# Another order for the last chunks of a layer stack, and another way through the "weighted values" stage, in a seven-part transformer kernel

## The reference

```python
x = x + attn_a(ln(x))        # softmax(x x^T) x over 2048 tokens
x = x + ffn(ln(x))           # 2 layers: local attention + gated feed-forward
x = x + attn_b(ln(x))        # "weighted values"
x = x + ffn(ln(x))           # the same 2 layers, the same weights

def attn_b(x):
    q, k, v = split(x @ qkv_w)                       # 128 columns each
    mq, mk  = mean(q), mean(k)                       # per token
    s_qk, s_q2, s_k2 = sums of products of (q-mq), (k-mk) / 127
    A = (((2*mq*mk+c1)*(2*s_qk+c2)) / ((mq**2+mk**2+c1)*(s_q2+s_k2+c2)+1e-7))**2
    h = relu(groupnorm(conv3(A), 2 groups of 2 channels) * gn_g + gn_b)
    A = A + conv3(h) + conv2_b
    weights = softmax(sigmoid(A), over tokens)
    ch_w = sigmoid(relu(mean_tokens(x) @ ch_w1 + ch_b1) @ ch_w2 + ch_b2)
    return (weights[..., None] * v * ch_w) @ proj_w + proj_b
```

## Time and profile before

| what | us |
|---|---|
| median of 3 runs (range) | 1821.97 (1821.23 to 1822.14) |
| the profiled execution, its own time | 1820.76 |
| its span, first to last instruction | 1819.0 |
| TensorE, VectorE, ScalarE, GpSimd busy in the span | 1613.2, 1284.9, 1202.6, 1175.3 |
| mean granted TensorE clock, as a share of 2.4 GHz | 0.945 |

### The profile page before, as it was taken

How to read it: one execution, slowest core, us unless ns; L and a number is a source line. 1 busy time by engine, 2 the same in 40 slices (tenths; PEclk the granted TensorE clock), 3 DMA queues, 4 the chain that set the end, 5 groups by cost and what they waited for, 6 DMA issues and landing times.

```text
span 1819.0 us, 47842 instructions
## 1 busy us (share of the span) xinstructions
PE 1613.2 (89%) x20074; PEld 1259.1 (69%) x20074; DVE 1284.9 (71%) x1689; ACT 1202.6 (66%) x1870; POOL 1175.3 (65%) x772
## 2 busy tenths in 40 slices
PE   4999978999999999999866666999999999999974
PEld 2777847877777777777644544877777777777763
DVE  4776658888787878788724455988787877888841
ACT  5876855677677776667655435677767777776753
POOL 3010028988888888888633115988888888888842
PEclk8999988999999999999986577999999999999997
DMA  3100002222222222222100001222222222222111
GB/s 91 41 8 1 1 23 53 65 57 55 51 55 48 58 48 62 49 51 55 31 9 1 0 6 37 68 54 58 49 60 52 55 57 49 57 49 53 42 28 46
DMA packets 66145, 78.87 MB, mean 43 GB/s; under 512 B 14146, under 2 KB 41868, under 8 KB 65932
## 3 DMA queue, kind: packets, MB, share of 16 engines
q1 hardware_dynamic: 65932, 75.82, 17.2%
HBM read 23.10 MB, written 2.10 MB: 14 GB/s over the span
## 4 chain that ended last, share of the span: by engine, by line
PE 61%; ACT 17%; DVE 13%; issue 4%; POOL 3%; DMA 1%; DVEq 0%; POOLq 0%; SPq 0%; ACTq 0%
PE PS L190 9%; PE PS L192 8%; PE PS L191 7%; PE PS L706 7%; PE PS L687 4%; DVE t L976 3%; PE PS L610 3%; PE PS L662 3%; ACT t L900 2%; PE PS L669 2%; ACT L922 2%; ACT L900 2%; DVE t L982 2%; ACT t L846 2%; PE PS L1171 2%
## 5 line engine op out<-in xcount | busy, mean ns | idle before, releaser
L1104 POOL TENSOR_TENSOR t<-t 128x1024 f32<-128x1024 f32 x128 | 427.3, 3339 | 109.9 <-DVE t L982 109.8
L1110 POOL TENSOR_TENSOR t<-t 128x512 f32<-128x512 f32 x256 | 321.6, 1278 | 18.4
L1128 POOL TENSOR_TENSOR HL<-t,HH 114x512 fp32r<-114x512 f32 (+1 forms) x96 | 130.0, 1367 | 141.1 <-ACT HH L906 141.1
L1032 DVE TENSOR_TENSOR yT<-PS,yT 128x128 f32<-128x128 f32 x128 | 37.3, 292 | 234.1 <-PE PS L706 233.8
L190 PE MATMUL PS<-wqh,HH 128*128 128x512 f32 x384 | 175.1, 456 | 30.0 <-DVE t L982 18.2
L846 ACT ACTIVATE t<-PS 128x1024 f32<-128x1024 f32 x128 | 131.3, 1026 | 90.4 <-PE PS L669 90.0
L993 DVE TENSOR_TENSOR t<-t 128x1024 f32<-128x1024 f32 x128 | 183.9, 1437 | 4.5
L814 ACT ACTIVATE t<-PS 128x1024 f32<-128x1024 f32 x128 | 131.2, 1025 | 72.1 <-PE PS L192 72.1
L1003 DVE TENSOR_TENSOR t<-PS,t 128x1024 bf16<-128x1024 f32 x128 | 155.9, 1218 | 19.9 <-ACT t L831 9.1
L976 DVE TENSOR_REDUCE t<-t 128x16 f32<-128x1024 f32 x128 | 154.8, 1210 | 17.1 <-ACT t L814 16.8
L1015 DVE TENSOR_REDUCE t<-PS 128x8 bf16<-128x1024 f32 x128 | 155.6, 1215 | 1.2 <-PE PS L636 1.2
(11 more groups left out here) (219 smaller groups left out, 3872.3 us busy)
## 6 DMA issues: line engine op xcount, KB each, us to landing
t<-t SPq DMA_DIRECT2D x254, 130.0 KB, 2.3
t<-in_c_rope SPq DMA_DIRECT2D x128, 128.0 KB, 2.7
t<-yT SPq DMA_DIRECT2D x112, 128.0 KB, 2.4
t<-in_L_attn_a_x SPq DMA_DIRECT2D x4, 512.0 KB, 6.8
out_x<-t SPq DMA_DIRECT2D x8, 256.0 KB, 2.8
t<-yT SPq DMA_DIRECT2D x16, 127.8 KB, 2.3
t<-in_L_ffn_wqkv SPq DMA_DIRECT2D x2, 768.0 KB, 4.3
t<-in_L_ffn_w SPq DMA_DIRECT2D x2, 341.0 KB, 3.4
```

Of the source, the lines that this page charges most:

```text
L1104: e.e.tensor_tensor(BL.tc.rearrange("p (x h) d -> p x h d", x=2), BL.qn.rearrange("p (x h) d -> p x h d", x=2), sin.to_broadcast([128, 2, ...
L1110: e.e.tensor_tensor(tv[:, :, 32 * s:32 * s + 32], tv[:, :, 32 * s:32 * s + 32], BL.tc[:, :, 32 * (1 - s):32 * (1 - s) + 32], ALU.add).then ...
```

## The change

**Layer stack (both times).** STEPS becomes TS + 4 = 68, and what is left of chunks A, B and Z is written out on each engine in an order of its own, with more banks of PSUM (0 to 7) and with the low halves made by VectorE. The gelu reads the gate from PSUM with its bias, without the copy `gate`. The second matmul waits for each of the three pieces of its operand by itself. The second layer's result is added straight into x1, and the residual add of GpSimd no longer adds that result but yT as it stands after attention; it moves from 17 steps late to 12, and for B and Z behind the loop.

```diff
-        STEPS = 4 * (NC - 1) + 16 + 2
+        STEPS = TS + 4
...
+            def second(C, bank):
-                e.wait_ge(S.ff_lo, 3 * (NC * u + C) + 3)
                 for i in range(3):
+                    e.wait_ge(S.ff_lo, 3 * (NC * u + C) + i + 1)
...
+            second(A, 7)
+            first(B, 2, 1, 6, S.ff_g)
+            first(B, 0, 0, 3, S.ff_l)
+            first(B, 1, 0, 2, S.ff_l)
+            first(B, 2, 0, 0, S.ff_l)
+            centred(Z)
+            second(B, 4)
+            variance(Z, 1)
+            for i, bank in enumerate((3, 2, 0)):
+                first(Z, i, 1, bank, S.ff_g)
+            first(Z, 0, 0, 5, S.ff_l)
+            first(Z, 1, 0, 6, S.ff_l)
+            first(Z, 2, 0, 7, S.ff_l)
+            second(Z, 4)
```

ScalarE's order behind its loop:

```diff
+            gelus(B, range(2))
+            high_for_feed_forward(Z)
+            gelu_there(B, 2, 6)
+            e.e.preload_act_table_set("natural_log_exp_and_others")
+            high_hidden(B, 0)
+            high_hidden(B, 1)
+            square(Z)
+            high_hidden(B, 2)
+            deviation(Z, 1)
+            e.e.preload_act_table_set("gelu_and_others")
+            high_normed(Z)
+            for i, bank in enumerate((3, 2, 0)):
+                gelu_there(Z, i, bank)
+            for i in range(3):
+                high_hidden(Z, i)
```

VectorE's order behind its loop, and GpSimd's residual adds:

```diff
+            add_second(A, 7)
+            e.e.tensor_tensor(fed(HL, Z), BL.ysf, fed(HH, Z).bitcast(F32), ALU.subtract).then_inc(S.sf_lo, 1)
+            gated(B, 0, 3)
+            gated(B, 1, 2)
+            low_hidden(B, 0)
+            gated(B, 2, 0)
+            low_hidden(B, 1)
+            low_hidden(B, 2)
+            scaled(Z)
+            e.e.tensor_tensor(fed(HL, Z), BF.nf, fed(HH, Z).bitcast(F32), ALU.subtract).then_inc(S.nh_lo, 1)
+            add_second(B, 4)
+            gated(Z, 0, 5)
+            gated(Z, 1, 6)
+            low_hidden(Z, 0)
+            gated(Z, 2, 7)
+            low_hidden(Z, 1)
+            low_hidden(Z, 2)
+            add_second(Z, 4)
...
-                if chunk_at(s, 17) is not None and chunk_at(s, 17) >= NCH:
-                    add_residual(chunk_at(s, 17))
+                if chunk_at(s, 12) is not None and chunk_at(s, 12) >= NCH:
+                    add_residual(chunk_at(s, 12))
+            add_residual(NC - 2)
+            add_residual(NC - 1)
```

```diff
-            normed_act(e, 5, 2, 2, x1, False)
+            normed_act(e, 5, 2, 2, x1, 1)
-            normed_dve(e, 5, 2, 2, x1)
+            normed_dve(e, 5, 2, 2, x1, value_weights_dve)
```

```diff
+                    halves(e.e, PS[:, j % 4, 256 * s:256 * s + 256], h, hl, BV.wceh.rearrange("p a b -> p (a b)"),
+                           BV.wcel.rearrange("p a b -> p (a b)"))
+                    mm = halves(e.e, PS[:, 7, 4 * j + 2 * s:4 * j + 2 * s + 2], h, hl, BV.wmh, BV.wml)
...
+            e.wait_ge(S.wv_ch, WVC["relu"])
+            neighbours(BW.h4.rearrange("p a b -> p (a b)"), 4)
+            for c in range(NCH):
+                if c >= 3:
+                    e.wait_ge(S.wv_z, c - 3 + 1)
+                halves(e.e, PS[:, c % 3, :], BW.Mh[c // 4], BW.Ml[c // 4], chunk(HH, c), chunk(HL, c)).then_inc(S.wv_x, 1)
+            e.wait_ge(S.wv_ch, WVC["sums"])
+            e.e.matmul(PS[:, 5, 16:18], avg, sm[:, 22:24], start=True, stop=True, skip_group_check=True).then_inc(S.wv_gm, 1)
+            e.wait_ge(S.wv_ch, WVC["end"])
+            e.wait_ge(S.wv_z, NCH)
+            for c in range(NCH):
+                for j in range(4):
+                    mm = e.e.matmul(PS[:, c, 128 * j:128 * j + 128], BW.w[:, 6, t:t + 1].to_broadcast([128, 128]), ident,
+                                    start=True, stop=True, skip_group_check=True)
```

ScalarE from the first group mean on:

```diff
+            e.e.activation(sm[0:32, 10:12], PS[0:32, 6, 0:2], ACT.Relu, bias=vec[0:32, 8:9], scale=1.0 / N).then_inc(S.wv_sg, 1)
             e.wait_ge(S.wv_cw, 2)
+            e.e.activation(sm[:, 20:22], PS[:, 6, 8:10], ACT.Sigmoid, bias=vec[:, 7:8]).then_inc(S.wv_sg, 1)
             e.e.preload_act_table_set("natural_log_exp_and_others")
+            for b in range(NB):
+                e.e.activation(BW.wpc[b], wp[:, :], ACT.Copy, scale=sm[:, 20 + b:21 + b])
+            e.wait_ge(S.wv_ch, WVC["var"])
+            e.e.activation(sm[:, 24:32], sm[:, 12:20], ACT.Ln, bias=eps_ap, scale=1.0 / 32).then_inc(S.wv_ga, 1)
+            e.e.activation(sm[:, 24:32], sm[:, 24:32], ACT.Exp, scale=-0.5).then_inc(S.wv_ga, 1)
...
+            for c in range(NCH):
+                e.wait_ge(S.wv_x, c + 1)
+                e.wait_ge(S.wv_sum, NCH)
+                e.e.copy(BW.P[c], PS[:, c % 3, :]).then_inc(S.wv_z, 1)
+                if c == 3:
+                    e.wait_ge(S.wv_ch, WVC["ode"])
+                    e.e.activation(w[:, 4, :], w[:, 3, :], ACT.Sigmoid, bias=vec[:, 44:45]).then_inc(S.wv_sg, 1)
+                    e.e.preload_act_table_set("natural_log_exp_and_others")
+                    e.wait_ge(S.wv_sg, 3)
+                    e.e.activation(w[:, 5, :], w[:, 4, :], ACT.Exp).then_inc(S.wv_ex, 1)
```

VectorE's last loop:

```diff
+                    e.wait_ge(S.wv_bs, c + 1)
+                    e.e.tensor_tensor(BW.P[c], PS[:, c, :], BW.P[c], ALU.mult).then_inc(S.wv_pw, 1)
+                if c % 2 == 0 and c:
+                    e.e.tensor_tensor(chunk(x1, c - 1), chunk(x1, c - 1), BW.P[c - 1], ALU.add)
```

More of the change, by code:

```diff
@@ L317, in rest @@
             def rest(c):
-                if twice:
+                if twice is not None:
                     e.wait_ge(S.ln_put, NCH * k + c + 1)
@@ L772, in feed_forward @@
                 if chunk_at(s, 10) is not None:
[L773 removed]
+                    variance(chunk_at(s, 10), 7)
             for s in range(STEPS):
@@ L1161, in weighted_values_pe @@
+        WVC = dict(base=14)
+        WVC["mean0"] = WVC["base"] + 5 + 1
+        WVC["ych"] = WVC["mean0"] + 1
+        WVC["mean1"] = WVC["ych"] + 5
+        WVC["var"] = WVC["mean1"] + 2
+        WVC["relu"] = WVC["var"] + 4
+        WVC["ode"] = WVC["relu"] + 7
+        WVC["sums"] = WVC["ode"] + 1
+        WVC["end"] = WVC["sums"] + 2
+        TT = NB * NT
+        STATS = TT // 2
         def weighted_values_pe(e, stage):
             others_ended(e, stage)
-            TT = NB * NT
-            e.wait_ge(S.wv_w, 3)
@@ L1187, in neighbours @@
                 mm.then_inc(S.wv_nb, 1)
-            sm = BW.sm
+            for j in range(STATS):
+                statistics(j)
+            e.wait_ge(S.wv_dd, STATS)
+            e.e.transpose(PS[:, 0, 0:128], wb[:, 256:384], ident).then_inc(S.wv_v, 1)
             e.wait_ge(S.wv_ch, WVC["base"])
@@ L1272, in build @@
-        WVC["relu"] = WVC["var"] + 4 + 4 + 1
-        WVC["ode"] = WVC["relu"] + 12
-        WVC["chm"] = WVC["ode"] + 2
-        WVC["chr"] = WVC["chm"] + 1
-        WVC["sums"] = WVC["chr"] + 1
-        WVC["end"] = WVC["sums"] + 4
+            for j in range(STATS):
+                dv = BW.dd[j % 3].rearrange("p (a c) b -> p a c b", c=2)
+                e.wait_ge(S.wv_dd, j + 1)
+                e.wait_ge(S.wv_rd, j - 3 + 1)
+                e.e.tensor_tensor(BW.dm[j % 3], dv[:, :, 0, :], dv[:, :, 1, :], ALU.mult).then_inc(S.wv_dm, 1)
@@ new lines, in weighted_values_dve @@
+            follow(v.tensor_tensor(h4, h4, h6, ALU.add))
+            follow(v.tensor_reduce(sm[:, 0:8], cb(h4), AX.X, ALU.add))
+            assert steps[0] == WVC["mean0"]
+            e.wait_ge(S.wv_sum, NCH)
+            follow(v.tensor_reduce(sm[:, 8:10], BW.ysum.rearrange("p (b c) -> p b c", b=NB), AX.X, ALU.add))
+            assert steps[0] == WVC["ych"]
+            e.wait_ge(S.wv_gm, 1)
+            for i in range(2):
+                follow(v.tensor_reduce(four(sm[:, 12:20], i), pair(PS[:, 5, 0:8]), AX.X, ALU.add))
@@ L1352, in weighted_values_dve @@
+            follow(v.scalar_tensor_tensor(cb(h4), eight(sm[:, 12:20]), -1.0 / 32, cb(h4), ALU.mult, ALU.add))
+            follow(v.tensor_tensor(h5, h4, h4, ALU.mult))
+            follow(v.tensor_reduce(sm[:, 0:8], cb(h5), AX.X, ALU.add))
+            assert steps[0] == WVC["mean1"]
+            e.wait_ge(S.wv_gm, 2)
+            for i in range(2):
+                follow(v.tensor_reduce(four(sm[:, 12:20], i), pair(PS[:, 5, 8:16]), AX.X, ALU.add))
             assert steps[0] == WVC["var"]
             e.wait_ge(S.wv_ga, 2)
-            for g in range(2):
-                for b in range(NB):
-                    hv = g5(h4)[:, g, :, b, :]
-                    follow(v.tensor_scalar(hv, hv, sm[:, 12 + 2 * g + b:13 + 2 * g + b], None, ALU.mult))
```

367 lines of the change are left out of this document (182 added, 185 removed).

## The result

The changed kernel takes 1782.0 us (median of 4 runs, 1781.6 to 1782.7), the kernel before 1822.1 us beside it: ratio 0.978 (95% interval 0.9766 to 0.9795), 40.0 us less. The forecast was 1780. The profiled execution has a span of 1779.9 us (its own time 1781.6, mean granted clock 0.951); the one of before had 1819.0.

What follows compares the result with a forecast made beforehand. TensorE, busy 89% of the span, was taken as close to the limit, so edits pay only through waits. Gains 32.2 + 4.5 + 5.5 = 42.2 us cut the span from 1819.0 to 1776.8, median 1780; range 1772 to 1788 (70%).

Steps and rivals of the forecast that it cites:

- End of a stack: Drain of the last chunks, twice: new order reaches the output transposes at about 1792.2, not 1808.3; 32.2 us for two (27 to 36).
- The first stack ends in the same way: End of the first stack: assumed like the second's, so the gain of 16.1 us a stack was counted twice.
- Residual add in the loop: GpSimd's add in the tile loop: 0.56 us each for ten adds hidden by an earlier wait; 4.5 us taken (0 to 5.6).
- Stage 5: Layer norm before the weighted values: double work and seven weight instructions make the statistics start 9.6 us later (8.5 to 10.5).
- Statistics: Weighted values' token tiles at 1.2 GHz: six steps of 0.213 us make 1.28 a tile, as before; gain 0.
- rival B: Statistics run at 2.4 GHz, a round takes 1.28 us instead of 2.56: 20 us less, 1760; 8%.
- E: Statistics' 256-column high or low matmuls take 0.85 us instead of 0.21: 61 us more, 1841; 3%.
- Chain: Small steps between statistics and last loop: 71 become 42 but wider, ending at 27.0 us instead of 28.9; 1.9 gained (0 to 4).
- rival D: Stages 5 and 6 lose: GpSimd's bias adds slow VectorE's chain steps and the last loop; 10 us more, 1790; 8%.
- that copy ends 3.3 us after the convolutions: In the chain: ScalarE's fourth eviction of P, which the weights' sigmoid stands behind, ends 3.3 us after the convolutions.
- Last loop: Final loop of the weighted values: 11.9 us instead of 25.1; gain 13.2 us (8.5 to 15.6).
- Rival C: Stack ends gain half: low clock and hand-overs of 0.2 us at some 25 steps lose 8 a stack, 1796; 10%.

Runs made afterwards that it cites:

- after_again: The changed kernel once more, unedited, as base for other runs: 1781.7 us (1781.1 to 1785.4), ratio 0.978.
- res_only: Kernel before with only GpSimd's residual add moved from 17 to 12 steps late, the second layer's result added into x1: 1811.9 us, ratio 0.995.
- weights_late: Changed kernel with VectorE's seven weight steps after its last normalised chunk of the third layer norm, not before its first: 1781.5 us, ratio 0.978.
- merged: Changed kernel with the two mean columns put behind the 256 centred columns, three matmuls of 258 columns per statistics tile: 1760.2 us, ratio 0.966.
- bias_early: Changed kernel with GpSimd's projection bias adds made between its products of the statistics, not beside VectorE's chain: 1780.7 us, ratio 0.978.
- warm: Changed kernel with 16 unread matmuls on TensorE behind the last chunk's variance at each stack end: 1777.3 us, ratio 0.976.
- best_warm: Changed kernel with merged, bias_early, later layer-norm casts, spread weight steps, earlier Z cast, 16 filler matmuls per stack end, earlier sigmoid: 1745.9 us, ratio 0.959.
- weighted_only: Kernel before with the new third layer norm and weighted values, old stack end and late residual add: 1817.2 us, ratio 0.998.

## Why the prediction was right

"Taken" is what the prediction put into its sum, "walk" its step-by-step order of a stack's end.

**End of a stack.** The walk gave 23.4 us from the cast of Z's shifted chunk to the end; the timeline has 23.85 in the first stack and 23.93 in the second. The points on the way fit too: the last matmul for B ends after 7.1 us (7.0 in the walk), Z's normalised low half after 12.0 (12.3). Some of this closeness is luck with the clock: the profile of `after_again`, the same kernel at 1785.4 us, needs 25.89 and 25.94, with a mean granted clock of 0.80 over this stretch and not 0.86. Forecast 32.2 us for both ends, measured 29.0. The step that failed is "The first stack ends in the same way": the 15.5 us of the second stack are close to the forecast's 16.1, but in the first the old order needed only 37.4 us from that cast and not 39.5, so 13.5 were gained. Windows of the kernel before, 19.5 and 22.4 us behind the last add of each stack:

```profile
945.00:955.00 10.00, 5.67 (x22) 3.57 (x21) 2.16 (x3) 6.73 (x9) 0.42 (x1) 0.99 0.00 0
...
1788.00:1798.00 10.00, 6.01 (x17) 3.48 (x16) 2.16 (x3) 6.06 (x8) 0.88 (x1) 0.82 0.00 0
```

The first end had TensorE at 2.4 GHz again from 945.2 on, 19.7 us behind its last add; the second only from 1791.7, 26.1 us behind. The prediction read one end and doubled it.

**Residual add in the loop.** Taken 4.5; measured 2.4 us a stack (`res_only`, second stack), so 4.8. Four tiles took 41.09 as where no add is, so the wait of the earlier trace rows hid it, and nothing of the deduction for the new neighbours came. The table's -4.0 and -0.8 are this 2.4 each, with 1.5 us more and less: a stretch of 1.2 GHz at tile 63 lay in the first stack before (921.3 to 924.7) and in the second after (1738.0 to 1741.4).

**Stage 5.** Taken 9.6 later, measured 9.2. `weights_late` shows that moving the seven steps behind the last chunk wins nothing: they end the stage themselves there.

**Statistics.** Taken 0, and 0 it was: a round of 2.56 us at clock 0.50, which is two tiles of six steps of 0.213. Rivals B and E fall. `merged` tests the model where it forecasts a difference, three steps in place of six, and it holds: 21.5 us, 20.5 expected.

The Trainium skill, page "TensorE: Matmul & The Clock Gate", section "LDWEIGHTS (loading the stationary operand)", gives columns / 1.2 ns, by which an estimate for such a load is 107 ns. The trace does not agree: loads start 213 ns apart at the granted clock of 0.50, also behind matmuls of 2 columns. In `merged` at 1.00 they start 121 ns apart. By the Trainium skill's section "Why this matters for your kernels" on the same page, to keep TensorE busy brings it to full clock, and rival B would have held. The trace after does not agree either: 15 us of 15 busy, and 0.50.

**Chain.** Taken 1.9 gained, measured 2.6; here two terms failed and nearly cancelled, which was luck. The prediction has the convolutions end 18.0 us after the chain's start; they ended after 19.9, since GpSimd's bias adds slowed VectorE's small steps (0.73 us for L1447, 0.19 without them); `bias_early` has 17.9. This is rival D's mechanism, with 2 us and not 10. And the prediction has "that copy ends 3.3 us after the convolutions"; it ended 0.7 after (1044.3, where the table load starts, against 1043.65), because TensorE was at 2.4 GHz again from 1041.6, inside the projected chunks, and because the convolutions were late. What stands behind it, two table loads and the eighth chunk, came as the walk had it.

**Last loop.** Taken 13.2, measured 13.0. VectorE's first three products start 1.64 us apart (1052.23, 1053.87, 1055.52), at the low clock, and its add is last, as in the walk.

**Stages 5 and 6 together**: 5.5 taken, 6.5 measured. **Rival C** (hand-overs that eat half of the ends, 8 us a stack) falls with the walk's error of 0.5 us, and of 2.5 in `after_again`. The sum was 42.2 us and the spans say 39.1: 3.2 too much at the ends and 0.9 at the start, where nothing was changed, 1.0 too little in stages 5 and 6. The median stood 0.4 above the profiled execution and not 1.2 as before, so 1780 missed by 2.

## What to carry to other kernels

Walk the new order of a drain instruction by instruction with durations from the trace, hand-overs included; it came within 0.5 us of 24 in one execution and within 2.5 in another. Then do the same for every place in which the old order occurs, for the same order can differ by 2 us from itself through the clock. When steps are moved under a cover, compare the cover's end with the moved steps' end and not with their sum, and when a matmul has few columns, count its weight load: at 1.2 GHz two columns more in a matmul that is there anyway cost 0.002 us (0.215 for 0.213), a matmul of their own costs as much as one of 256.

## What the runs showed of the hardware

- At 1.2 GHz a 128x128 weight load and its matmul take a slot of 0.213 us each time, whether the matmul has 256 columns or 2 (loads in the trace after; `merged` against the changed kernel: 22.4 us less in stages 5 and 6). At 2.4 GHz, with 258 columns, the slot is 0.121 us (`merged`).
- TensorE busy without a gap for 41 us stayed at 1.2 GHz, while in `merged` it was granted 2.4 GHz for 13 us, busy 10.85 of them. What makes the difference the runs don't tell.
- Sixteen matmuls that nobody needs, in a gap of 4.2 us, kept 2.4 GHz through both stack ends of the profiled execution of `warm` (2.2 and 2.7 us shorter), and through one of the two in `best_warm`; the medians fell by 4.4 and 4.3 us. One of the four executions of `warm` gained nothing.
- A VectorE step of 128x32 on SBUF took 0.73 us beside GpSimd's add of 128x512, and 0.19 without it; a cast of two columns 1.23 us beside GpSimd's subtraction.
- The kernel before and `res_only` have a second level, 15 to 17 us lower at a mean clock higher by 0.008 (6 of 56 and 2 of 12 executions); none of 52 executions of kernels with the new end of a stack has it, and none of 12 of `weighted_only`.
